# Linear attention with batch norm on one core: 32-wide tiles, PSUM banks by table, written call lists

## The reference

```
q, k, v = Wq x, Wk x, Wv x               per image, by 1x1 projection
k       = softmax(k) over the 16 channels of a head, for each pixel
context = k v^T                          per image and head, 16x16
out     = context^T q                    per image and head
y       = Wo out + x
result  = gamma (y - mean) / sqrt(var + 1e-5) + beta     mean, var over images and pixels
```

## Time and profile before

| | us |
|---|---|
| median of 3 runs | 49.64 (49.45 to 49.71) |
| the profiled execution | 49.98 |
| its span, first to last instruction | 48.7 |
| PE busy | 37.5 (77%) |
| VectorE busy | 34.5 (71%) |
| ScalarE busy | 27.1 (56%) |
| GpSimd busy | 18.5 (38%) |

### The profile page before, as it was taken

The page is one execution under the profiler, slowest core; times in us unless marked ns, Lnnn a source line. Parts: engine busy times, 40 slices in busy tenths (PEclk is TensorE's granted clock), DMA queues, the critical chain, the costliest instruction groups (busy, mean ns, idle before and its releaser), DMA issues.

```text
span 48.7 us, 1096 instructions
## 1 busy us (share of the span) xinstructions
PE 37.5 (77%) x377; PEld 32.5 (67%) x377; DVE 34.5 (71%) x90; ACT 27.1 (56%) x61; POOL 18.5 (38%) x28
## 2 busy tenths in 40 slices
PE   3999996869999999999999999999999930000000
PEld 3999994668887689898888979788787910000000
DVE  0019399799999958984996799793636697998000
ACT  0933550999787991593388079844634942910000
POOL 5830027399999959853017006281000000000000
PEclk9999999999999999999999999999999999555555
DMA  0398789710000000000000000000000000089995
GB/s 0 95 275 299 276 272 372 285 64 0 0 13 0 0 0 0 0 0 7 0 13 7 0 0 0 0 0 0 0 0 0 13 0 0 0 317 396 397 393 219
DMA packets 2597, 4.52 MB, mean 93 GB/s; under 512 B 416, under 2 KB 1184, under 8 KB 2592
## 3 DMA queue, kind: packets, MB, share of 16 engines
q1 hardware_dynamic: 2448, 4.33, 24.8%
q10 hardware_dynamic: 144, 0.13, 0.8%
HBM read 2.36 MB, written 2.10 MB: 91 GB/s over the span
## 4 chain that ended last, share of the span: by engine, by line
PE 59%; DVE 12%; DMA 12%; ACT 3%; SPq 3%; issue 2%; ACTq 0%
PE banks L425 17%; DMA x_sb<-x_dram 12%; PE banks L498 10%; PE banks L450 10%; PE banks L465 10%; PE banks L482 8%; DVE y_sb L407 7%; PE banks L479 4%; SPq L215 3%; DVE stats L380 3%; ACT x_hi L277 1%; DVE mean_var L389 1%; ACT v_sb L288 1%; ACT probs L282 1%; ACT std L309 1%
## 5 line engine op out<-in xcount | busy, mean ns | idle before, releaser
L263 POOL TENSOR_TENSOR probs<-probs,k_inv 128x256 f32<-128x256 f32 (+1 forms) x11 | 8.9, 822 | 8.6 <-DVE k_inv L354 8.6
L255 POOL TENSOR_TENSOR x_lo<-x_sb,x_hi 128x512 fp32r<-128x512 f32 (+1 forms) x7 | 7.8, 1124 | 5.2 <-ACT x_hi L277 5.2
L425 PE MATMUL banks<-wkv_hi,x_hi 128*128 128x256 f32 x32 | 7.2, 306 | 0.6 <-ACT v_sb L288 0.6
L277 ACT ACTIVATE x_hi<-x_sb 128x256 fp32r<-128x256 f32 (+1 forms) x11 | 5.4, 512 | 3.8 <-DMA x_sb<-x_dram 3.8
L425 PE MATMUL banks<-wkv_hi,x_lo 128*128 128x256 f32 x32 | 6.7, 290 | 0.5 <-POOL x_lo L255 0.5
L335 DVE TENSOR_REDUCE k_max<-banks 128x16 f32<-128x256 f32 (+1 forms) x11 | 5.7, 528 | 1.6 <-PE banks L425 1.5
L298 ACT ACTIVATE a_hi<-banks 128x256 fp32r<-128x256 f32 (+1 forms) x9 | 3.3, 361 | 6.2 <-PE banks L482 6.2
L425 PE MATMUL banks<-wkv_lo,x_hi 128*128 128x256 f32 x32 | 6.5, 283 | 0.0
L348 DVE TENSOR_REDUCE k_sum<-probs 128x16 f32<-128x256 f32 (+1 forms) x11 | 5.6, 532 | 0.5 <-ACT probs L282 0.4
L425 PEld LDWEIGHTS banks<-wkv_hi,x_hi 128*128 128x128 f32 x32 | 4.9, 192 | 1.5 <-issue 1.1
L342 DVE TENSOR_TENSOR probs<-banks,k_max 128x256 f32<-128x256 f32 (+1 forms) x11 | 5.6, 529 | 0.0
(11 more groups left out here) (42 smaller groups left out, 57.7 us busy)
## 6 DMA issues: line engine op xcount, KB each, us to landing
x_sb<-x_dram SPq DMA_DIRECT2D x5, 256.0 KB, 5.8
out_dram<-y_sb SPq DMA_DIRECT2D x2, 512.0 KB, 3.0
out_dram<-y_sb SPq DMA_DIRECT2D x3, 256.0 KB, 3.1
x_sb<-x_dram SPq DMA_DIRECT2D x1, 512.0 KB, 6.9
x_sb<-x_dram SPq DMA_DIRECT2D x2, 128.0 KB, 2.5
out_dram<-y_sb SPq DMA_DIRECT2D x2, 128.0 KB, 2.0
w_sb<-w_dram ACTq DMA_DIRECT2D x1, 128.0 KB, 2.7
w_sb<-w_dram SPq DMA_DIRECT2D x1, 128.0 KB, 5.7
```

The costliest lines, as they stand in the source:

```text
L255: nc.gpsimd.tensor_tensor(x_lo[:, p, px], x_sb[:, p, px], x_hi[:, p, px].bitcast(F32), ALU.subtract).then_inc(x_lo_ready, hi - lo)
L263: nc.gpsimd.tensor_tensor(heads, heads, inv.to_broadcast([128, (hi - lo) * CH * HEADS, D]), ALU.mult).then_inc(probs_ready, hi - lo)
L277: nc.scalar.activation(x_hi[:, p, px], x_sb[:, p, px], ACT.Copy).then_inc(x_hi_ready, hi - lo)
L425: last = nc.tensor.matmul(kv_ps(p)[:, g, :], xs[:, p, g * 128:(g + 1) * 128], ws[:, :], start=start and g == CH * image, stop=stop, skip_g ...
```

## The change

- T goes from 64 to 32: context and times_wo use four tiles of 32 channels in place of two of 64. The second image of a pair is shifted by one tile: its context is written 32 partitions on, and times_wo multiplies it with woT_turned, Wo rolled by 32 rows, loaded as a fifth part of w. The two images' u go to two banks.
- Banks come from the tables KV_BANK, CT_BANK, A_BANK and Y_BANK. Waits for a bank to come free are written in the list as `pe.wait_ge`.
- run_slots goes. Each engine has a written list of calls, by image range. TensorE projects image by image. All other stages go by pairs, but for single images at the start.
- SPLIT_BY_VECTOR = 0: GpSimd makes all low halves of x.
- x and the output lie in memory as (pair, channel, two images x pixel); a four-image transfer has 2 KB rows.
- One statistics call a pair, eight in all (COUNTS = 8, before nine).

```diff
-T = 64
+T = 32
-EXTRA = 2
-LAST = PAIRS - 1
-IN_PSUM = PAIRS - 3
-LO_BY_VECTOR = 2
+KV_BANK = [1, 0, 2, 3, 5, 6, 0, 1, 2, 3, 6, 7, 0, 1, 6, 7]
+CT_BANK = {0: 4, 2: 1, 4: 4, 6: 3, 8: 2, 10: 0, 12: 5, 14: 4}
+A_BANK = {0: 5, 2: 2, 4: 5, 6: 4, 8: 1, 10: 1, 12: 6, 14: 3}
+Y_BANK = {0: 3, 2: 3, 4: 2, 6: 6, 8: 7, 10: 2, 12: 7, 14: 5}
+SPLIT_BY_VECTOR = 0
+COUNTS = 8
+COPIED = 10
...
-                    sp.dma_start(w_sb[:, 2 * C:4 * C], w[:, 2 * C:4 * C]).then_inc(wqo_landed, 16)
+                    sp.dma_start(w_sb[:, 2 * C:5 * C], w[:, 2 * C:5 * C]).then_inc(wqo_landed, 16)
...
+def context(lo, hi):
+                            to = (t + (image - lo) * T) % C
+                            last = nc.tensor.matmul(ct[to:to + T, :], v_sb[:, image * CH + g, t:t + T],
+                                                    probs[:, image * CH + g, t:t + T], start=(g == 0),
+                                                    stop=(g == CH - 1), tile_position=(0, to), skip_group_check=True)
...
+def times_wo(lo, hi):
+                    wo = woT_turned if image > lo else woT
+                        to = (t - (image - lo) * T) % C
+                        last = nc.tensor.matmul(u[to:to + T, :], ct_sb[t:t + T, image, :], wo[t:t + T, :],
+                                                start=True, stop=True, tile_position=(t, to), skip_group_check=True)
```

More of the change, by code:

```diff
@@ L167, in attention_batchnorm @@
         y_view = y_sb[:, :, :].rearrange("c p (b n) -> c (p b) n", n=N)
[L169 to L182, removed]
@@ new lines, in piece_of, with kv_ps, ct_ps @@
+        def piece_of(image):
+            return next(i for i, (lo, hi) in enumerate(PIECES) if lo <= image < hi)
+        def kv_ps(lo, hi):
+            if hi - lo == 1:
+                return banks[:, KV_BANK[lo], :].rearrange("n (g c) -> n g c", g=CH)
+            return banks[:, KV_BANK[lo]:KV_BANK[lo + 1] + 1:KV_BANK[lo + 1] - KV_BANK[lo], :].rearrange(
+                "n i (g c) -> n (i g) c", g=CH)
+        def ct_ps(lo, hi):
+            return banks[:, CT_BANK[lo], 0:(hi - lo) * T]
@@ L268, in scalar_program @@
+            normalise(1, 2)
+            split_lo(8, 9)
+            split_lo(9, 10)
+            split_lo(10, 12)
+            split_lo(12, 13)
+            normalise(2, 4)
+            normalise(4, 6)
+            split_lo(13, 14)
+            split_lo(14, 16)
+            normalise(6, 8)
+            normalise(8, 10)
+            normalise(10, 12)
+            normalise(12, 14)
+            normalise(14, 16)
         def scalar_program(act):
             act.dma_start(w_sb[:, 0:2 * C], w[:, 0:2 * C]).then_inc(wkv_landed, 16)
[L271 to L277, removed]
@@ L301, in copy_y, with copy_u @@
[L301 to L306, removed]
+            def copy_u(lo, hi):
+                act.wait_ge(u_ready, hi)
+                nc.scalar.activation(u_sb[:, lo:hi, :], u_ps(lo, hi), ACT.Copy).then_inc(u_copied, hi - lo)
@@ new lines, in scalar_program @@
+            exponentials(0, 1)
+            copy_values(0, 1)
+            copy_values(1, 2)
+            exponentials(1, 2)
+            split_hi(6, 7)
+            split_hi(7, 8)
+            split_hi(8, 9)
+            copy_values(2, 4)
+            exponentials(2, 4)
+            split_hi(9, 10)
+            copy_values(4, 6)
+            split_hi(10, 12)
+            exponentials(4, 6)
+            split_hi(12, 13)
+            split_hi(13, 14)
+            copy_values(6, 8)
+            exponentials(6, 8)
@@ new lines, in scalar_program @@
+            split_hi(14, 16)
+            copy_values(8, 10)
+            exponentials(8, 10)
+            copy_u(0, 2)
+            copy_values(10, 12)
+            copy_u(2, 4)
+            exponentials(10, 12)
+            split_a_hi(0, 2)
+            copy_y(0, 2)
+            split_a_hi(2, 4)
+            copy_u(4, 6)
+            copy_values(12, 14)
+            exponentials(12, 14)
+            copy_u(6, 8)
+            copy_u(8, 10)
+            exponentials(14, 16)
+            split_a_hi(4, 6)
@@ new lines, in vector_program @@
+            shift_keys(8, 10)
+            largest_keys(10, 12)
+            mask_context(2, 4)
+            shift_keys(10, 12)
+            sum_heads(6, 8)
+            sum_heads(8, 10)
+            mask_context(4, 6)
+            invert_sums(6, 8)
+            invert_sums(8, 10)
+            split_a_lo(0, 2)
+            sum_heads(10, 12)
+            largest_keys(12, 14)
+            invert_sums(10, 12)
+            count_y(0, 2, 0)
+            shift_keys(12, 14)
+            split_a_lo(2, 4)
@@ new lines, in vector_program @@
+            mask_context(6, 8)
+            largest_keys(14, 16)
+            mask_context(8, 10)
+            shift_keys(14, 16)
+            sum_heads(12, 14)
+            mask_context(10, 12)
+            invert_sums(12, 14)
+            sum_heads(14, 16)
+            split_a_lo(4, 6)
+            invert_sums(14, 16)
+            split_a_lo(6, 8)
+            split_a_lo(8, 10)
+            count_y(2, 4, 1)
+            count_y(4, 6, 2)
+            count_y(6, 8, 3)
+            mask_context(12, 14)
@@ L389, in vector_program @@
+            mask_context(14, 16)
+            count_y(8, 10, 4)
+            split_a_lo(10, 12)
+            split_a_lo(12, 14)
+            split_a_lo(14, 16)
+            count_y(10, 12, 5)
+            count_y(12, 14, 6)
+            count_y(14, 16, 7)
+            dve.wait_ge(y_counted, COUNTS)
             nc.vector.bn_aggr(mean_var[:, :], stats[:, :]).then_inc(aggregated, 1)
@@ L410, in tensor_program, with project @@
         def tensor_program(pe):
[L411 to L413 removed]
+            def project(image):
+                if image == 0:
                     pe.wait_ge(w_hi_ready, 1)
[L415 to L437 removed]
@@ L439, in context, with pass_over @@
-            def context(p, lo, hi):
-                pe.wait_ge(probs_ready, 2 * p + hi)
-                pe.wait_ge(v_ready, 2 * p + hi)
-                if p >= 1:
-                    pe.wait_ge(ct_masked, 2 * p)
-                for image in range(lo, hi):
-                    ct = ct_ps(p, lo, hi)[:, (image - lo) * T:(image - lo + 1) * T]
+                pe.wait_ge(x_hi_ready, image + 1)
+                def pass_over(xs, ws, start, stop):
+                    for g in range(CH):
+                        last = nc.tensor.matmul(kv_ps(image, image + 1)[:, g, :], xs[:, image, g * 128:(g + 1) * 128],
+                                                ws[:, :], start=start and g == 0, stop=stop, skip_group_check=True)
+                    return last
```

404 lines of the change are left out of this document (240 added, 164 removed).

## The result

The changed kernel takes 46.61 us in the median of four runs (46.24 to 46.84), the kernel before 49.67; the ratio is 0.938 (95% interval 0.932 to 0.945). Forecast were 46.0 us and 44.5 to 48.4. All ratios here are of undisturbed executions alone and the medians of all executions, so the two don't always rank alike. The profiled execution took 46.64 us with a span of 45.3, against 49.98 and 48.7.

A forecast was written before the change was run, and what follows sets the result against it. TensorE's work, its losses before 10.16 us and the tail set the time; the aggregate comes 3.7 us sooner, stores cost 0.1, so span 48.7 becomes 45.1, profiled execution 46.4, median 46.0 us, range 44.5 to 48.4.

The forecast's parts named there:

- The sum: Whole kernel: 3.7 us gained to the aggregate less 0.1 for stores, 3.6; span 45.1, median 46.0.
- Call order: TensorE's list: 13 changes of tile shape in place of 28, 0.15 us each, 2.25 us less.
- Narrow tiles: Context matmuls on TensorE: four 32-wide tiles share the array, 0.24 us saved a pair, 1.9 us in all.
- wo at four slots, 0.44: Wo matmuls of a pair on TensorE: four slots of 0.11 us, the same 0.44 as before.
- the rival that I gave 0.08: Wo matmuls: all eight tiles share the array, 0.22 us a pair, 1.3 less after 17.6, total 44.8; chance 0.08.
- The Trainium skill's rule against small matmuls: Context on TensorE: about 60 cycles however small a matmul, so 32 would take 0.8 us against 0.23 forecast.
- The start, 17.6 us: Up to TensorE going on at 17.6 us: 13 images done, 2.6 us lost, half a microsecond more than before.
- From 17.6 on: TensorE after the start: 17.45 us of work plus 0.4 of waits, ending at 35.45; VectorE close but not the bound.
- The tail and the stores: Kernel end: only 0.69 us of statistics after the last pair's matmuls, aggregate at 36.4; 2 KB store rows cost 0.1.
- The signs: Trace checks: chain on TensorE, first context near 11.1, first wo near 16.3, aggregate near 36.4, stores near 400 GB/s.
- Context at 0.93 or 0.47 a pair: Two context rivals: one matmul every 0.029 us, total 50.3, chance 0.06; no more sharing than now, 50.1, chance 0.05.
- Waiting lists: Engines' fixed lists: waits of some 0.3 us at six or seven places, 2 us go, total 48.0; chance 0.13.

The follow-up runs named there:

- e8: Changed kernel with times_wo of images 8 and 9 moved behind times_wq of 4 and 5, two more tile-shape changes: 47.36 us, ratio 0.941 to the old kernel.
- e3: Changed kernel with the second image not turned, on the same tiles as the first and multiplied with plain woT: 47.43 us, ratio 0.956 to the old kernel.
- e2: Changed kernel with T = 64, narrow tiles alone undone: 47.40 us, ratio 0.956 to the old kernel.
- e7: Old kernel with T = 32 alone, second image on the same tiles, u in one bank: 49.12 us, ratio 0.986 to the old kernel.
- e1: Changed kernel again with no edit, as base for its chip: 46.65 us, ratio 0.933 to the old kernel.
- e4: Changed kernel with the low halves of images 0 and 1 made by VectorE: 46.36 us, ratio 0.935 to the old kernel.
- e5: Changed kernel with the old memory layout of x and the output: 47.31 us, ratio 0.948 to the old kernel.
- e10: Changed kernel with the old memory layout of x and the output, repeated on another chip: 47.56 us, ratio 0.938 to the old kernel.
- e12: Changed kernel with two low halves on VectorE, old output layout, and times_wq of images 2 and 3 before project 15: 46.66 us, ratio 0.941 to the old.
- e11: Changed kernel with w in 2 KB rows, turned Wo loaded by two small extra DMAs: 46.56 us, ratio 0.931 to the old kernel.

## Why the prediction was right, point by point

- **The sum.** The forecast span 45.1 was 45.3, the aggregate 36.4 was 36.55, the profiled execution 46.4 was 46.64. Of the median's miss of 0.61 us 0.24 is in that execution and 0.37 in the offset: the forecast put the median 0.4 below the profiled execution, because the old one lay 0.34 below, and the new one lies 0.03 below. In medians the change gave 3.06 us, not 3.6. That the aggregate came within 0.15 us is in part luck: the start was 0.72 late and the rest 0.57 short, and within the rest two wrong terms nearly cancel (below).
- **Call order.** 13 changes of shape for 28 is what the trace has. What one costs was confirmed roughly (0.12 in e8, 0.15 in e3's wo rows). How much of the 2.25 us, the largest term of the sum, arrived was not measured: no run takes the new order back. Of the 3.06, e2 and e3 account for 0.75 and 0.78 if the two add up, and order, start and tail share what is left, about 1.5. That this is the call order is argued, not shown.
- **Narrow tiles.** Four share the array, and a context pair lost 0.22 in the old kernel (e7) and 0.16 to 0.20 in the new one (e2), against 0.24 forecast. The term was mis-sized at the end of the path: 1.9 us forecast, 0.68 to 0.75 arrived in e2. The step that failed is that every saved 0.24 counts. Two of the contexts lie in a stretch that VectorE paces, and the first two in a start that TensorE doesn't set.
- **wo at four slots, 0.44.** Wrong, and the rival that I gave 0.08 was right: all eight tiles share the array, three pairs took 0.95 us, and undoing the turn cost 0.78. It made good about two thirds of the 1.2 us that the contexts fell short.
- **The Trainium skill's rule against small matmuls.** It didn't decide. 32 context matmuls take 0.39 (e7) to 0.46 us with their change of shape, not the 0.8 worked out from the 60 cycles of the Trainium skill's "TensorEngine Tiling (Array Packing)", section "Instruction Overhead", because four overlap.
- **The start, 17.6 us.** It was 18.32, 0.72 late. The chain names the piece of images 2 and 3: it landed at 6.26 us, where the old kernel converts it from 5.25 on, so GpSimd had pair 4-5 done at 9.47 and not at 8.4. My walk took every x piece to land as before. In e1, e4 and e5 the chain runs over the piece of images 4 and 5 instead. wkv_lo took 0.996 us in place of 0.42, because GpSimd now subtracts beside it, but that isn't on this chain, and e4 shows that it cost the end nothing with x landing as late as it did.
- **From 17.6 on.** 18.8 us forecast to the aggregate, 18.23 measured; wo was faster. "VectorE is not the bound, though close" was wrong between 21.8 and 24.1: the chain runs over it and TensorE waits 0.35:

```profile
24.14 0.82 PE L547 MATMUL banks<-probs,v_sb 128*32 128x32 f32 x64 [0.35 <-DVE a_lo L422]
```

- **The tail and the stores.** "Only the last pair's 0.69 comes after its matmuls" came true by a hair, with VectorE's three statistics and TensorE's last matmul ending together. 8.7 us forecast behind the aggregate's start, 8.76 measured; the 2 KB rows cost 0.16 (7.50 against 7.34 in e5 and e10, 7.33 in e12), with 0.12 worked out and 0.1 taken.
- **The signs.** "The chain still on TensorE" failed: the chain is on TensorE for 37% of the span, 59% before. The first context came at 12.10, not 11.1, and wo of the first pair at 17.27, not 16.3, both by the late start.
- **The rivals.** Context at 0.93 or 0.47 a pair: neither. Waiting lists: the pause of 0.35 us before 24.14, not 2.

Open is why the x pieces of images 2 to 5 come late in the changed kernel. With the old layout of x images 2 and 3 come nearly as early as before and images 4 and 5 later than ever (two traces, e5 and e10); the old pitch of w (e11) brings neither back. Both old at once, with everything else new, weren't tried.

## What to carry to other kernels

A stage that gets shorter on the bound engine gives its gain back where it covered somebody else's copy: look at what the next stage waits for before counting it (e7: 0.22 a pair arrived only while projections lay between). Small matmuls pay when they land on different tiles, by rows and columns; turning the second image by one tile, with its u in a bank of its own, was worth as much as halving the tile. An engine's duration from the trace of before holds only while its neighbour does what it did there. And before a slow instruction is blamed, look whether the chain passes over it: wkv_lo more than doubled and cost the end nothing, because x came late.

## What the hardware showed that I had not expected

- A VectorE subtraction with two SBUF inputs, 128x256: 996 ns beside a GpSimd subtraction, 426 without.
- Eight fp32 matmuls on 32x32 tiles, two in each row group, in two banks: all start within 0.07 us, and wo of a pair of images, two such groups, takes 0.32 us in a run of three pairs.
- Four 64x64 tiles, turned the same way, take the same time for wo: 0.60 for two pairs in e2 and in the changed kernel.
- The same x load, images 4 and 5, is converted at 6.22 us in one kernel, 7.21 in another and 8.03 in a third, and neither the layout of x nor the pitch of w by itself explains it.
- In one execution (e10) projection matmuls took 0.22 us each in place of 0.12 from 5.36 to 10.28 us, with the granted clock at 1.00 in those rows.
